# Four cross-attention layers on one core: VectorE's queue in the second wide layer, the first jobs of wide and narrow layers, and unread products on TensorE

## The reference

```python
# L0: narrow heads (16 of 16), layernorm on x and context, biases, then a gelu feed-forward
x = x + attention(ln(x) @ wq + bq, ln(ctx) @ wk + bk, ln(ctx) @ wv + bv) @ wo + bo
x = x + gelu(ln(x) @ w1 + b1) @ w2 + b2
# L1: wide heads (16 of 64), RMS norm on x, no scale, no biases
x = x + attention(rms(x) @ wq, ctx @ wk, ctx @ wv) @ wo
# L2: wide heads, rotary positions on queries and keys, mask over keys, layernorm behind
x = ln(x + attention(rope(x @ Wq), rope(ctx @ Wk), ctx @ Wv, mask) @ Wo)
# L3: narrow heads again, layernorm on x and context, biases
x = x + attention(ln(x) @ Wq + bq, ln(ctx) @ Wk + bk, ln(ctx) @ Wv + bv) @ Wo + bo
```

## Time and profile before

| | us |
|---|---|
| median of 3 executions | 2081.63 |
| their range | 2077.27 to 2087.77 |
| the profiled execution, own time | 2082.45 |
| its span in the trace | 2080.7 |
| PE busy | 1949.8 (94%) |
| DVE busy | 1442.7 (69%) |
| ACT busy | 1294.6 (62%) |
| POOL busy | 563.5 (27%) |

### The profile page before, as it was taken

The page is one execution under the profiler, slowest core; times in us unless marked ns, Lnnn a source line. Parts: engine busy times, 40 slices in busy tenths (PEclk is TensorE's granted clock), DMA queues, the critical chain, the costliest instruction groups (busy, mean ns, idle before and its releaser), DMA issues. The chain is left out here.

```text
span 2080.7 us, 50431 instructions
## 1 busy us (share of the span) xinstructions
PE 1949.8 (94%) x18664; PEld 1675.9 (81%) x18664; DVE 1442.7 (69%) x2900; ACT 1294.6 (62%) x3250; POOL 563.5 (27%) x676
## 2 busy tenths in 40 slices
PE   6899996979999999999999999999999998999997
PEld 5777775978888888888887888888888877787775
DVE  5777875545555555555578899889889974677775
ACT  3777775646556556556566666666666653677775
POOL 3323320000000000000056666766666651000000
PEclk9999998989999999999999999999999998899998
DMA  5544432102000000000001000000000001344441
GB/s 165 155 130 141 143 117 73 57 30 83 15 9 9 16 8 9 16 9 8 16 2 53 10 17 10 10 16 10 9 11 17 1 1 46 110 130 128 135 127 57
DMA packets 72858, 109.61 MB, mean 53 GB/s; under 512 B 7052, under 2 KB 62508, under 8 KB 72620
## 3 DMA queue, kind: packets, MB, share of 16 engines
q1 hardware_dynamic: 72332, 105.88, 16.6%
q10 hardware_dynamic: 288, 0.51, 0.1%
HBM read 69.18 MB, written 37.19 MB: 51 GB/s over the span
## 5 line engine op out<-in xcount | busy, mean ns | idle before, releaser
L1531 ACT ACTIVATE wide_P<-PS,MX 100x361 f32<-100x361 f32 x512 | 281.1, 563 | 179.8 <-DVE MX L1655 179.8
L615 ACT ACTIVATE L_P<-PS,MX 100x361 f32<-100x361 f32 x512 | 253.0, 566 | 122.3 <-DVE MX L745 122.3
L745 DVE TENSOR_REDUCE MX<-PS 100x2 f32<-100x722 f32 x256 | 219.8, 900 | 47.0 <-PE PS L501 46.9
L1655 DVE TENSOR_REDUCE MX<-PS 100x2 f32<-100x722 f32 x256 | 220.2, 900 | 15.3 <-PE PS L1398 14.9
L1661 DVE COPY wide_PT<-PS 128x300 f32<-128x300 f32 x256 | 117.6, 460 | 141.9 <-PE PS L1405 141.8
L513 PE MATMUL PP<-CON,L_P 100*128 100x100 f32 x1536 | 186.3, 259 | 25.5 <-DVE L_PT L752 16.5
L513 PEld LDWEIGHTS PP<-CON,L_P 100*128 100x128 f32 x1536 | 153.1, 146 | 47.7 <-ACT L_P L615 33.6
L1405 PEld LDWEIGHTS PS<-CON,wide_P 100*128 100x128 f32 x1536 | 159.7, 140 | 24.8 <-ACT wide_P L1531 3.3
L1843 POOL TENSOR_TENSOR wide_AC<-wide_T,wide_COSM 128x362 f32<-128x362 f32 x128 | 130.2, 1017 | 178.9 <-ACT wide_T L1480 125.2
L1405 PE MATMUL PS<-CON,wide_P 100*128 100x100 f32 x1536 | 175.9, 249 | 1.4 <-ACT wide_P L1531 1.0
L1505 ACT ACTIVATE wide_V<-PJ 128x512 f32<-128x512 f32 (+1 forms) x126 | 75.6, 600 | 147.0 <-PE PJ L1317 147.0
(11 more groups left out here) (242 smaller groups left out, 5401.9 us busy)
## 6 DMA issues: line engine op xcount, KB each, us to landing
strips<-L_KS SPq DMA_DIRECT2D x256, 90.5 KB
L_KA<-strips SPq DMA_DIRECT2D x64, 362.0 KB, 3.1
C<-ctx_t SPq DMA_DIRECT2D x32, 361.0 KB, 3.0
kept<-L_CTH SPq DMA_DIRECT2D x16, 361.0 KB, 4.8
kept<-L_CTL SPq DMA_DIRECT2D x16, 361.0 KB, 5.6
L_CTH<-kept SPq DMA_DIRECT2D x16, 361.0 KB, 4.2
L_CTL<-kept SPq DMA_DIRECT2D x16, 361.0 KB, 5.0
C<-in_ctx SPq DMA_DIRECT2D x8, 256.0 KB, 3.4
```

The source lines that it names most:

```text
L615: nc.scalar.activation(P[:, (4 * g + j) % 8, 0:SK], PSB[0:SQ, j, 0:SK], ACT.Exp, bias=MX[:, s % 2, 4 * q + j:4 * q + j + 1], scale=1.0).th ...
L745: nc.vector.tensor_reduce(MX[:, s % 2, 4 * q + 2 * i:4 * q + 2 * i + 2], PSB[0:SQ, 2 * i:2 * i + 2, 0:SK], AX.X, ALU.max, negate=True).the ...
L1531: nc.scalar.activation(P[:, (2 * g + i) % 4, 0:SK], score_bank(g, i)[0:SQ, 0:SK], ACT.Exp, bias=MX[:, s % 2, h:h + 1], scale=1.0, accum_ou ...
L1655: nc.vector.tensor_reduce(MX[:, s % 2, 2 * p:2 * p + 2], PSB[0:SQ, 2 * (g % 2):2 * (g % 2) + 2, 0:SK], AX.X, ALU.max, negate=True).then_in ...
```

## The change

**Second wide layer and unloads.** An unload is now done by one engine for a whole pair: DVE the even pairs (128 x 600), ACT the odd ones, each waiting for both turns. DVE's `invert` stands ahead of the joins. The low half of rotated queries goes from DVE to POOL, after the rotations of the slot's keys and before that of its query. ACT makes only the first rotated high half before the slot's first copies and the other two behind them.

**Wide start.** Context 0 is loaded in the feed-forward block. The weights of L1 are split in smaller chunks (K 256, 256, 512; Q 512, 512), FIRST has four keys ahead of X, and ACT's and DVE's order of splits and jobs follows.

**Narrow start.** W1 moves behind the keys, K(1, 0) into slot (0, 0), C10 and C11 ahead of the values, `keep(0)` ahead of the load of context 3 and of `strips(1, 0)`.

**Unread products.** `keep_busy` issues products of 128 x 128 columns whose result nobody reads: 6, 4 and 2 at the start of L0, 4 in each of the six slots (15, 1) to (16, 2) of L0 and L3, 9 at L0's end, 12, 7 and 8 in the feed-forward block, 9 at the wide block's beginning and 4 and 14 in its last two slots.

```diff
+        def keep_busy(dst, n):
+            for _ in range(n):
+                nc.tensor.matmul(dst[:, 0:128], ident, CON[:, 0:128], start=True, stop=True)
...
-            FIRST = ([("W", 0, 0)] + ctx0 + [("W", 0, 1), ("K", 0, 0), ("K", 0, 1), ("X", 0, 0)] + [("Q", 0, t) for t in range(4)]
-                     + [("V", 0, 0), ("V", 0, 1)] + ctx1 + [("K", 1, 0)])
+            FIRST = ([("W", 0, 0)] + ctx0 + [("K", 0, 0), ("X", 0, 0), ("K", 0, 1), ("W", 0, 1)] + [("Q", 0, t) for t in range(4)]
+                     + ctx1 + [("V", 0, 0), ("V", 0, 1)])
...
                     if first:
+                        keep(0)
                         sp.wait_ge(Z["c_normed"], 2)
                         load_context(sp, 3, CS[1], s_c[1])
                     strips(1, 0)
                     if first:
-                        keep(0)
                         keep(1)
...
+                        if (B - 1, 1) <= (s, q) <= (B, 2):
+                            keep_busy(begin(("P" if q == 0 else jobs_at(s, q + 1)[0][0][0], s - 1, 0) if q < 3 else ("O", s - 1, 0)), 4)
+                    keep_busy(PSB[:, 3, :], 9 if first else 0)
...
                     load_output_weights(sp, "ffn")
+                    load_turned_context(sp, 0)
...
-            FIRST = [("X", 0, 0)] + [("K", 0, p) for p in range(HP)] + [("Q", 0, p) for p in (4, 5, 6, 7, 0, 1, 2, 3)] + [("X", 2, 0)] + [("V", 0, c) for c in range(3)]
+            FIRST = [("K", 0, p) for p in range(4)] + [("X", 0, 0)] + [("K", 0, p) for p in range(4, HP)] + [("Q", 0, p) for p in (4, 5, 6, 7, 0, 1, 2, 3)] + [("X", 2, 0)] + [("V", 0, c) for c in range(3)]
...
-            CHUNKS = [(0, "K", 0, 512), (0, "K", 512, 1024), (0, "Q", 0, 1024), (0, "V", 0, 512), (0, "V", 512, 1024),
+            CHUNKS = [(0, "K", 0, 256), (0, "K", 256, 512), (0, "K", 512, 1024), (0, "Q", 512, 1024), (0, "Q", 0, 512), (0, "V", 0, 512), (0, "V", 512, 1024),
...
-                        nc.scalar.activation(PT[:, (2 * g + 1) % 4, :], score_bank(g, 1)[:, 0:KV_TILES * SQ], ACT.Copy).then_inc(Z["unloaded_odd"], 1)
+                        nc.scalar.activation(PT[:, 2:4, :], PSB[:, 2:4, 0:KV_TILES * SQ], ACT.Copy).then_inc(Z["unloaded_second"], 1)
...
-                        for key in turns_of(G - 1):
+                        for key in turns_of(G - 1)[:1]:
                             rotated_high(key)
                         for key in first:
                             job(key)
-                        if s < NS:
-                            unload(2 * G)
+                        for key in turns_of(G - 1)[1:]:
+                            rotated_high(key)
...
-                        nc.vector.tensor_copy(PT[:, (2 * g) % 4, :], score_bank(g, 0)[:, 0:KV_TILES * SQ]).then_inc(Z["unloaded_even"], 1)
+                        nc.vector.tensor_copy(PT[:, 0:2, :], PSB[:, 0:2, 0:KV_TILES * SQ]).then_inc(Z["unloaded_first"], 1)
...
-                        for key in turns_of(G - 1):
-                            join(key)
                         if d == 0 and s:
                             invert(s - 1, 1)
                         if d == 2 and s < NS:
                             invert(s, 0)
+                        for key in turns_of(G - 1):
+                            join(key)
...
                         for key in turns_of(G - 1):
-                            rotated_low(key)
+                            if key[0] == "K":
+                                rotated_low(key)
...
                         for key in turns_of(4 * s + d):
-                            rotate(key)
+                            if key[0] == "K":
+                                rotate(key)
+                        for key in turns_of(4 * s + d - 1):
+                            if key[0] == "Q":
+                                rotated_low(key)
+                        for key in turns_of(4 * s + d):
+                            if key[0] == "Q":
+                                rotate(key)
```

124 lines of the change are left out of this document (74 added, 50 removed).

## The result

The changed kernel takes 2074.6 us (median), the kernel before 2082.0: ratio 0.9969, 95% interval 0.9958 to 0.9980. That is 6.5 us (4.2 to 8.7) where the sum had 27; the medians are 7.5 apart. One of the changed kernel's twenty executions took 4645.7 us and is not in the ratio.

A forecast was written before the change was run, and what follows sets the result against it. TensorE was taken to set the pace, with L2's VectorE and GpSimd chain sometimes ending last. Terms -6 (L2), -10.5 (wide start), -5 (L0), -3 (L3), -2.5 (ends, feed-forward) made -27: 2082.45 to 2055 us, range 2037 to 2069.

The forecast's parts named there:

- Wide start: Wide block's beginning: first key 3.8 us sooner, 3 us less waiting, 3.7 from the clock; -10.5 us (-7 to -14).
- L0 start: First narrow layer's start: bias product off the keys' way, PE's 3.31 us context wait gone; -5 us (-2 to -9).
- L3 start: Last narrow layer's start: the 3.55 us bias product moves, without the rest; -3 us (-1 to -7).
- L2: Second wide layer: shorter waits for RX and fewer slow-clock windows, less a new wait for QL; -6 us (-18 to +4).
- The wait for QL: L2, slots (s, 1) of even samples: PE waits 1.1 us for GpSimd's low query half; seven samples, +7.7 us (3.5 to 12).
- Odd slots d = 0: L2: inversion ahead of the joins lets the shuffle start sooner; 1.2 us each, -9.6 over eight odd samples.
- VectorE's pause of 1.09 us: L2, odd slots: VectorE's wait for GpSimd's query rotation, said to cover most of the moved inversion work.
- the three windows at 1.2 GHz: L2: slow-clock stretches behind waits for RX might go with shorter waits; 0 to -5.1 us, half taken, -2.5.
- Unread products: Ends of L0 and L3 and feed-forward: if they hold the clock, -2.5 us together (-6 to +2).
- QL free: Rival for L2: QL on GpSimd costs nothing, since it is done before the scores want it; 2044 us, chance 0.16.
- locks cost more: Rival for L2: VectorE and GpSimd exclude each other, even samples lose 2.5 instead of 1.1 us; 2068, chance 0.12.
- an end near 2075: Case of no change to be seen: L2 loses 8 and the starts gain half of what was taken; chance 0.04.

The follow-up runs named there:

- context1_ahead: The changed kernel with sample 1's turned context loaded ahead of L2's three weight matrices at the wide start; 2066.9 us, ratio 0.9930 to the kernel before.
- inv_ql_gpsimd: The kernel before with VectorE's inversion ahead of the joins, plus the low half of the queries on GpSimd; one execution, 2074.9 us.
- before_again: The kernel before, unchanged, run for a second profiled execution; 2085.2 us.

## Why the prediction was wrong

Forecast 2055 with a range of 2037 to 2069; measured 2074.6. The direction held, the size did not. What the sum lost is the wide start's 10.5 us, nearly all of the two narrow starts' 8 and the 2.5 of the unread products.

**Wide start: the step that failed is the last of it.** The first key came at 454.4 (3.0 us sooner after the block before, 3.8 forecast), the first scores 21.6 us behind it (29.5 before): -10.9 against -10.5, at a clock of 1.00 instead of 0.70. (Some of the 7.9 is luck: with the old wide start the first scores came 29.5 us behind the first key in three profiles, but 26.7, 26.7 and 25.2 in three others.) What the step did not ask is what stands behind the first scores. The step counted the way to the first scores as gain and put the sample behind them at 0. It never followed SP's queue: 3 MB of weights of L2 wait there for the last low split of L1's, and context 1 stands behind them. That split comes 27.3 us behind the feed-forward block (28.2 before), while the first scores came 10.9 us sooner. The kernel before was just in time (issued 10.5 us ahead of the first scores, 0.92 us of idling); with 0.4 us of lead PE idled 9.46 us and ran at 1.2 GHz for 10.2 us, and sample 0 took 10.9 us more. context1_ahead gets these 10.9 us back with the transfer moved and nothing else, so this is shown.

**L0 start: the same failure in small.** W1 and K(1, 0) did leave the way, first scores at 33.6 instead of 35.8. The price of `keep(0)` was put on the strips; what it and the strips really hold up is context 3, which VectorE awaits in order ahead of the maxima. Of the 2.2 us gained up to the first scores 2.0 fell into that wait (-0.2 at sample 1). On the mean of all profiles the new orders gain 1.5 us up to sample 1, where 5 were forecast, and are 2 us late at sample 15. The step that failed is that a sooner key was taken for a sooner sample 1. **L3 start:** -3 forecast, -0.3 on the mean of all profiles.

**L2: the term was near (-6 forecast, -8.8 measured), its parts were not.** The wait for QL was priced at 1.1 us and is 1.14 where it stands alone (inv_ql_gpsimd); in the changed kernel it is 0.5, since the slot before is longer. Odd slots d = 0 were given 1.2 us and gained 1.5 with the change (12.2 to 10.8, medians of samples 19 to 27), 1.8 with the inversion alone (10.5). Two steps were wrong. VectorE's pause of 1.09 us was taken as given and as cover; it came from the collision and goes with it. And even samples were put at 0, since "their sum stays": the sum of VectorE's own instructions did, but beside the table products RX took twice as long. In the sum, the odd samples 17 to 29 gained 10.8 us (9.6 forecast for eight), the even ones 18 to 28 lost 4.5 (7.7 forecast for seven), samples 30 and 31 gained 2.8 and sample 16 lost 0.3. Of the three windows at 1.2 GHz one is left, so half of them was a fair guess. That the term came near is the cancelling of these errors.

**Unread products:** -2.5 forecast, within the scatter of 0, and a cost of 3 to 4 us likely. That they hold the clock was right at L0's end and in front of the wide block, and not at L0's and L3's starts; that this pays was not right.

**The rivals.** None of them named the mechanism that decided: a transfer whose issue does not get sooner when its user does. The first (QL free, put at 2044, where its sum gives 2045) and the second (locks cost more) each held a part. The case that came true, an end near 2075, stood there with 0.04, for another reason.

**Scatter.** Differences of narrow stretches were read from one profile of each kernel; 3 to 5 us of them were scatter between executions, before_again shows.

## What to carry to other kernels

When the start of a stage gets shorter, ask for each input of the next step when it is issued, and behind what: a transfer that stands in a DMA queue behind a wait for some other engine's last piece of work stays where it is, however much sooner its user is ready. An engine's pause beside another's long instruction may be one and the same event, so a reordering that separates the two is worth the pause too, and work put into the pause can bring the collision back (QL on GpSimd: 9 us in L2). Edits of several in-order queues are not additive (4.2, 9 and 10.6 us of cost alone, 4.5 together), so each is to be measured alone and with the others, on stretches of the trace that do not scatter.

## What the runs showed of the hardware

One GpSimd product of 128 x 200 took 0.62 us alone and 1.69 beside VectorE's joins; one of 128 x 362 took 0.95 alone and 2.30 beside the inversion and the joins. The copy of RX took 0.46 us alone and 0.89 beside a table product. A transfer of 361 KB behind three of 1 MB was issued at 475.56 and let ACT go on at 485.08, 9.5 us later. TensorE's granted clock over the first 30 us was 0.69 to 0.96 with twelve unread products there and 0.93 to 1.00 without them. The median samples of wide layers repeat within 0.1 us from execution to execution, narrow stretches with their trips over DRAM differ by 3 to 5 us in 270.
